# Reordering loads and per-step work in the attention stage of a fused attention and int4 feed-forward kernel

## What is computed

```python
def attention(up, down, Wq, Wk, Wv, Wskip):        # up: layernorm(x), down: ctx
    q, k, v = Wq @ up, Wk @ down, Wv @ down
    energy = einsum('bcn,bcm->bnm', q, k) / sqrt(128)
    return Wskip @ up + einsum('bnm,bcm->bcn', softmax(energy), v)

def ffn(x, Wg, Wu, Wd):                             # int4 weights, dequantized in groups of 64
    return (silu(x @ Wg.T) * (x @ Wu.T)) @ Wd.T

x = x + attention(layernorm(x), ctx, Wq, Wk, Wv, Wskip)
x = x + ffn(layernorm(x), Wg, Wu, Wd)
```

## Time and profile before

| | |
|---|---|
| median of 3 runs | 1473.16 us (1472.75 to 1473.59) |
| profiled execution | 1472.75 us, span 1470.9 us |
| TensorE busy | 1453.8 us, 99% of the span |
| VectorE busy | 819.7 us, 56% |
| ScalarE busy | 635.9 us, 43% |
| GpSimd busy | 206.6 us, 14% |

### The profile page before, as it was taken

One profiled execution on the slowest core, in us unless ns is written; L12 is line 12 of the kernel. 1 busy time (PEld: TensorE's weight loads), 2 busy tenths in 40 slices (PEclk: granted clock), 3 DMA queues, 4 the chain that ended last, 5 costly groups with the idle time before them and its releaser, 6 DMA issues.

```text
span 1470.9 us, 18688 instructions
## 1 busy us (share of the span) xinstructions
PE 1453.8 (99%) x6774; PEld 716.2 (49%) x6774; DVE 819.7 (56%) x1175; ACT 635.9 (43%) x1189; POOL 206.6 (14%) x265
## 2 busy tenths in 40 slices
PE   8999999999999999999999999999999999999998
PEld 6777764444444444444444444444444444444443
DVE  5898977735734644644544544553553554463365
ACT  6889883334334334243343333433424433433320
POOL 1242321011011011011011111101101101101100
PEclk9999999999999999999999999999999999999999
DMA  5322222277377467558547638638637737737794
GB/s 160 120 83 87 90 86 58 48 153 142 59 137 142 78 113 146 97 88 165 103 71 171 114 57 181 119 46 169 122 60 157 130 57 152 135 58 155 135 336 172
DMA packets 47028, 174.82 MB, mean 119 GB/s; under 512 B 6672, under 2 KB 9488, under 8 KB 42640
## 3 DMA queue, kind: packets, MB, share of 16 engines
q0 software_dynamic: 23040, 83.90, 35.0%
q1 hardware_dynamic: 23808, 90.20, 20.3%
q10 hardware_dynamic: 144, 0.26, 0.0%
HBM read 73.67 MB, written 100.66 MB: 119 GB/s over the span
## 4 chain that ended last, share of the span: by engine, by line
PE 93%; DVE 3%; ACT 3%; issue 1%; POOL 0%; DVEq 0%; POOLq 0%
PE ps L505 51%; PE ps L561 28%; PE ps L467 3%; PE ps L434 3%; PE ps L668 2%; PE ps L651 2%; PE ps L422 1%; PE ps L462 1%; PE ps L456 1%; ACT temps L706 1%; ACT temps L720 1%; DVE neg_max L1044 0%; PE ps L410 0%; PE ps L412 0%; ACT xt L713 0%
## 5 line engine op out<-in xcount | busy, mean ns | idle before, releaser
L505 PE MATMUL ps<-xt,w_gu 128*128 128x512 f16 x3528 | 789.0, 379 | 0.0
L505 PEld LDWEIGHTS ps<-xt,w_gu 128*128 128x128 f16 x3528 | 345.1, 98 | 414.9 <-issue 0.6
L561 PE MATMUL ps<-w_d_all,h_all 128*128 128x512 f16 x1920 | 440.5, 379 | 0.0
L820 ACT ACTIVATE stage<-ps,pow 128x512 f32<-128x512 f32 x320 | 219.8, 687 | 413.8 <-PE ps L561 413.8
L561 PEld LDWEIGHTS ps<-w_d_all,h_all 128*128 128x128 f16 (+1 forms) x1920 | 187.8, 98 | 226.6
L382 POOL DMA_DIRECT2D out<-stage x160 | 138.6, 866 | 1029.5 <-ACT stage L820 1029.5
L1187 DVE TENSOR_TENSOR temps<-ps,temps 128x512 f32<-128x512 f32 x42 | 29.0, 691 | 211.0 <-PE ps L505 211.0
L807 ACT CAST h_all<-temps 128x512 f16<-128x512 f32 x42 | 25.8, 613 | 131.0 <-DVE temps L1206 131.0
L1192 DVE TENSOR_TENSOR temps<-ps,temps 128x512 f32<-128x512 f32 x42 | 29.0, 691 | 95.1 <-PE ps L505 95.1
L1196 DVE TENSOR_TENSOR temps<-ps,temps 128x512 f32<-128x512 f32 x42 | 28.9, 689 | 75.8 <-PE ps L505 75.8
L1200 DVE TENSOR_TENSOR temps<-ps,temps 128x512 f32<-128x512 f32 x42 | 28.9, 688 | 75.2 <-PE ps L505 75.2
(11 more groups left out here) (114 smaller groups left out, 1284.5 us busy)
## 6 DMA issues: line engine op xcount, KB each, us to landing
out<-stage POOLq DMA_DIRECT2D x160, 512.0 KB, 5.3
grid<-grids SPq DMA_DIRECT2D x136, 256.0 KB, 4.9
raw<-packed SPq DMA_DIRECT2D x22, 512.0 KB, 3.6
out<-stage SPq DMA_DIRECT2D x17, 512.0 KB, 2.9
stage<-x SPq DMA_DIRECT2D x13, 512.0 KB, 3.5
raw_d<-packed SPq DMA_DIRECT2D x12, 512.0 KB, 7.9
xt<-out SPq DMA_DIRECT2D x12, 512.0 KB, 10.4
out<-xt SPq DMA_DIRECT2D x12, 512.0 KB, 2.6
```

The costliest lines, as they stand in the source:

```text
L505: mm = pe.matmul(bank, w_gu[e][:, wp, w, P * j:P * j + P], xt[:, xb, xp, j, cols], start=(fresh and n == 0), stop=(n == 3 * J - 1), skip_g ...
L561: mm = pe.matmul(ps[:, 6 + oh, :], h, w, start=(n == 0), stop=(n == len(products) - 1))
L820: act.activation(stage[:, t % STAGES, NOUT * oh:NOUT * oh + NOUT], ps[:, 6 + oh, :], ACT.Copy, scale=pow2[:, 10:11]).then_inc(s_stage, 1)
```

## The change

On SP, the six loads of scales and zeros and the first weight job's loads are issued right behind the loads of batches 0 and 1, ahead of those of batch 2. On ScalarE, `normalize_probs(i, 0)` moves ahead of the "between" block's `block_hi`, and in step 0 `keys_out(1)` moves behind `exponentials(0, 1)`. On VectorE, `maxima(i, 1)` moves ahead of the "between" block's `block_lo`, and in step 0 it moves behind `x_arrived(2)` and `row_stats(0, 2)`. TensorE's and GpSimd's lists stay as they are.

```diff
@@ sync
-            for i in range(B):
+            load_batch(0)
+            load_batch(1)
+            for k in range(3):
+                sp.dma_start(grids_all[:, k, :], scales[k, :, :]).then_inc(s_grids_in, 16)
+                sp.dma_start(grids_all[:, 3 + k, :], zeros[k, :, :]).then_inc(s_grids_in, 16)
+            load_raw(0, 0)
+            load_grid(0, 0)
+            for i in range(2, B):
                 load_batch(i)
-                if i == 2:
-                    for k in range(3):
-                        sp.dma_start(grids_all[:, k, :], scales[k, :, :]).then_inc(s_grids_in, 16)
-                        sp.dma_start(grids_all[:, 3 + k, :], zeros[k, :, :]).then_inc(s_grids_in, 16)
-                if i == 4:
-                    load_raw(0, 0)
-                    load_grid(0, 0)
                 if i >= 4:
                     store_batch(i - 4)
@@ scalar, step(i)
                 if i < B:
                     exponentials(i, 0)
+                    normalize_probs(i, 0)
                 for unit in blocks_of_step(i, "between"):
                     block_hi(unit)
-                if i < B:
-                    normalize_probs(i, 0)
                 if i >= 1:
                     probs_out(i - 1, 1)
                 if i % 2 == 0:
                     for unit in blocks_of_step(i, "after"):
                         block_hi(unit)
-                if i == 0:
-                    keys_out(1)
                 if i < B:
                     exponentials(i, 1)
...
-                if 0 < i < B - 1:
+                if i + 1 < B:
                     keys_out(i + 1)
@@ vector, step(i)
                 if i + 2 < B:
-                    if i == 0:
-                        maxima(0, 1)
                     x_arrived(i + 2)
                     row_stats(0, i + 2)
+                if i < B:
+                    maxima(i, 1)
                 for unit in blocks_of_step(i, "between"):
                     block_lo(unit)
-                if 0 < i < B:
-                    maxima(i, 1)
```

## The result

The changed kernel takes 1485.11 us in the median of six runs (1483.0 to 1487.07), the kernel before 1473.17 us (1472.32 to 1473.59). The ratio is 1.008, with a 95% interval of 1.0068 to 1.009: slower by 11.9 us. The profiled execution took 1484.24 us, its span is 1481.9 us.

What follows compares the result with a forecast made beforehand. TensorE, busy 1453.8 of 1470.9 us, bounds the kernel, so new waits are paid nearly in full. Front 6.3 + steps 3 to 9 5.0 + later steps 0.9 = 12.2 us on 1472.75 gives 1485; range 1478 to 1490.

Steps and rivals of the forecast that it cites:

- the forecast case: Late x delays the front 6.3 us and X22's bank waits add 5.0 + 0.9 us: 1485 us, chance 0.62.
- The late x: SP's load queue: x of batch 2 lands at 20.0 us, behind scales, zeros, raw weights and grid; bounds 16.2 and 21.
- the row of the late store: Trace row: first store, behind raw and grid, lands at 42.1 us; 2.1 MB in 9.7 us, used for x.
- The chain from x to the keys: Step 0, VectorE and ScalarE: statistics 1.44, maxima 1.26, exponentials 1.94, `keys_out` 0.36 us, to 25.1 us.
- The half clock: TensorE after idling from 19 to 25 us: `energies(1, 0)` at 1.2 GHz throughout, 3.46 us.
- The order of step 0: VectorE, x in time at 15.3 us: about 0.3 us lost, as statistics only change places with maxima.
- The odd steps: Steps 3 to 15: X22 waits 1.25 us for X21's bank; 5.0 us in steps 3 to 9, 0.9 later.
- The ScalarE edit: Moving `block_hi` of X21 behind a normalization costs nothing; without the maxima as cover, up to 1.7 us per odd step.
- Quick data: Rival: x of batch 2 lands near 15.3 to 16.2, front loses 0.3 to 2.5 us, 1479.4 to 1481.6; chance 0.14.
- free banks: Rival: X22's wait is covered and only the front counts, about 1479.5 us; chance 0.12.
- the chains of steps 13 to 16: Faster rival, ScalarE to TensorE: earlier maxima and normalizations give back waits, 1.6 us shown, 1468.6 to 1471.5; chance 0.03.

Runs made afterwards that it cites:

- run with filled idle time: Changed kernel with fourteen more matmuls of 128x128, result unread, on TensorE ahead of `energies(1, 0)`: 1481.97 us, ratio 1.0059.
- `extremes` behind and the filling: Kernel before with `extremes` directly behind `inverse_total(0, 1)` in step 0, GpSimd's reduction left in place, and 13 extra matmuls on TensorE: 1472.25 us, ratio 0.999.
- the filling alone: Kernel before with only 13 extra matmuls of 128x128 in TensorE's idle time ahead of `probs_transposed(0, 0)`: 1472.77 us, ratio 0.9997.

## Why the prediction was right

The median came out at 1485.11 us, forecast 1485 in a range of 1478 to 1490; the forecast case, both parts, is the one that happened. That the two numbers agree to 0.1 us is luck: the terms come to 10.95 us where 12.2 was forecast. By its steps:

- **The late x.** Forecast landing 20.0, bounds 16.2 and 21; measured 18.6. The scales and zeros were sized rightly: forecast 3.2 us, measured 10.3 - 7.1 = 3.2. What was too long is the rest: raw, grid, ctx and x were forecast at 9.7 + 0.4 us, less 0.6 for an overlap, and took 18.6 - 10.3 = 8.3 us. That is 2.23 MB at 268 GB/s, where the row of the late store gave 216. Why a load ends that row's pattern sooner than the store did is open. The estimate by the Trainium skill's HBM rate ("DMA: Bandwidth & Descriptors", Specifications), 16.5, is 2.1 us too early, so it is further off than the row. That raw and grid do it, and the scales and zeros alone don't, the run with the weights behind batch 4 shows.
- **The chain from x to the keys.** Forecast 5.1 us from landing to `energies(1, 0)`, measured 23.51 - 18.6 = 4.9.
- **The half clock.** Forecast for the energies (3.46 us; measured 27.08 - 23.51 = 3.57 until the next product), not for the product behind them, which took 1.71 us until the next in place of 0.86. This cancelled 0.96 of the 1.4 us by which x was early, again by luck: 28.79 measured where 29.4 was forecast. The run with filled idle time shows that the clock is a real part of the loss, 2.4 us in the profile. My expectations for the loads alone and for the loads as before left it out, and both were too low (1475.4 for 1478.34, 1478.9 for 1480.05).
- **The order of step 0.** Taken as 0.3 us with x in time; measured 1.6 us of late products, because the later keys leave TensorE idle and at half clock for the whole of the energies. The prediction's own chain, started at 15.3 us, gives 24.7 for the products, which is 1.6 us late; the 0.3 beside it did not follow from it.
- **The odd steps.** Forecast 1.25 us each, measured 1.13 us of idle time, 1.29 from the energies' start to X22, and 1.1 to 1.2 us of added lateness per step (1.0 in step 3). Steps 3 to 9 cost 4.4 us where 5.0 was forecast, and steps 11 to 16 kept 0.8 where 0.9 was forecast. Together 5.25 for 5.9, alone and in the change alike.
- **The ScalarE edit.** Forecast free in the change with a price without its cover: both hold for the move of `block_hi`, with about 2 us of price over all steps, where the prediction gave only an upper bound of 1.7 us per step. The move of `keys_out(1)` costs 0.5 us alone in the kernel before, which the prediction did not price by itself.
- **The rivals.** Quick data is refuted by the landing, free banks by the seven waits; nothing was given back at the chains of steps 13 to 16 beyond what absorbed X22's delay.

The sum of terms by the rows is 5.7 + 5.25 = 10.95 us, the median moved by 11.9. The remaining 1 us I can't place: 0.5 lies outside the span (1484.24 - 1481.9 = 2.34 against 1.85), the rest between the profiled execution and the median, whose runs spread over 4 us. The profiled execution was also 0.33 us ahead of the one before up to step 0 (TensorE's row of 16.83 stood at 17.16). The spread fits where the half clock falls. With the loads alone the runs spread over 6 us, and their mean granted clocks go with the times: 0.998 in the quickest (1475.44 us), 0.995 in the two slowest (1480.84 and 1481.59). With `extremes` behind and the filling the spread is 0.44 us, all at 0.999 or 1.0. No run changed the clock and nothing else.

## What to carry to other kernels

Before moving an instruction earlier on one engine, find the loop that its neighbour closes: here a PSUM bank is freed by a small subtraction, and putting a reduction that waits for TensorE ahead of it made TensorE wait for itself, seven times. A load that is "early" and not needed yet still costs whoever is issued behind it in the same queue; compare its landing with its first need, and the first need of what it displaces. Where an engine list is short of work at the start, price the stall and the half clock behind it.

## What the runs showed of the hardware

- 1.6 MB of weight loads and a 512 KB store behind them, 2.1 MB in all, took 9.7 us in the kernel before, 216 GB/s; a stretch of one microsecond shortly before (30.5 to 31.5 us) reached 369 GB/s. In the changed kernel 512 KB issued behind 2.6 MB landed 9.9 us after its issue, and the last 2.23 MB went at 268 GB/s.
- Half clock came in or just behind TensorE's waits of 3.66 us before the change, of 3.22 us with the loads alone, and of 2.26 us with the filling alone; with a wait of 1.19 us there (`extremes` behind and the filling) it did not come. The 13 added matmuls (26 records) in the first of these gaps kept the clock at 1.00 until 23 us.
- The first 20 matmul records of the kernel before take 421 ns in the median, as the filling's do at a granted clock of 0.50, and the filling's take 275 ns at 1.00; so TensorE starts the kernel at half clock, although the windows there read 1.00. The Trainium skill ("TensorE: Matmul & The Clock Gate", Part 1) says that the throttled state is the default and activity releases it; the trace agrees, with these 421 ns and with 0.50 until 29 us after the idle stretches that end at 16.83 and 23.51.
- GpSimd's reduction over partitions shows 0.40 us of busy time in the profile, but the next job on GpSimd started 8.2 us after its start (32.95 to 41.15) with `extremes` late, and 7.0 us after it in the kernel before (24.56 to 31.57), each time with nothing shown that it waited for.
